# Sentinel rows written once ahead, and last expert tiles that overlap their neighbour

## The reference

```python
h = tok(x)                       # convolution over 5 frames, relu, batch norm over all rows
h = h + attn(layernorm(h))       # 8 heads, 121 keys per sequence, a column bias from 8192 edges
h = h + ffn(layernorm(h))        # below

logits = xf @ Wr + br            # xf: 3872 x 128, 8 experts
idx = top_1(logits)              # the gate is softmax over one value, so 1
for e in range(8):               # W1[e] 128 x 512, W2[e] 512 x 128
    oe = relu(xf @ W1[e] + b1[e]) @ W2[e] + b2[e]
    out = out + where(idx == e, oe, 0)
```

## Time and profile before

| | us |
|---|---|
| three runs | 348.50, 352.64, 356.53 |
| profiled execution | 345.34 |
| its span | 343.6 |
| PE busy | 275.7 (80%) |
| ACT busy | 227.0 (66%) |
| DVE busy | 225.4 (66%) |
| POOL busy | 213.2 (62%) |
| mean granted TensorE clock | 0.916 |

### The profile page before, as it was taken

The page is one execution under the profiler, slowest core; times in us unless marked ns, Lnnn a source line. Parts: engine busy times, 40 slices in busy tenths (PEclk is TensorE's granted clock), DMA queues, the critical chain, the costliest instruction groups (busy, mean ns, idle before and its releaser), DMA issues. The chain is left out here.

```text
span 343.6 us, 7885 instructions
## 1 busy us (share of the span) xinstructions
PE 275.7 (80%) x2139; PEld 215.0 (63%) x2139; DVE 225.4 (66%) x714; ACT 227.0 (66%) x843; POOL 213.2 (62%) x299
## 2 busy tenths in 40 slices
PE   3890969899999998897898879856008999999980
PEld 2660746556767665665656656545007999999970
DVE  2895676888988999877787686455403565656540
ACT  3851378889888998697897788640005777777740
POOL 7044554787766867888888886667721454545551
PEclk9995698999999999999999999895557999999996
DMA  3200990000000000001000100112634333333300
GB/s 94 79 2 1 303 281 18 0 2 1 3 0 2 1 3 15 16 15 32 15 24 23 31 15 17 30 31 73 171 98 122 93 101 109 94 104 108 91 13 0
DMA packets 15579, 19.15 MB, mean 56 GB/s; under 512 B 3960, under 2 KB 11676, under 8 KB 15537
## 3 DMA queue, kind: packets, MB, share of 16 engines
q1 hardware_dynamic: 11520, 11.73, 12.1%
q0 software_dynamic: 3296, 5.98, 6.0%
q10 hardware_dynamic: 720, 0.94, 0.9%
HBM read 10.69 MB, written 8.44 MB: 56 GB/s over the span
## 5 line engine op out<-in xcount | busy, mean ns | idle before, releaser
L467 ACT ACTIVATE P<-psS,nmax 121x121 f32<-121x121 f32 x256 | 88.9, 380 | 17.9 <-DVE nmax L709 17.2
L929 PE MATMUL psS<-patT,qT 128*121 128x484 f32 x128 | 64.3, 607 | 2.5 <-ACT P L467 1.7
L396 POOL DMA_INDIRECT out<-y_out,xg x38 | 36.9, 971 | 46.9 <-issue 31.5
L362 POOL TENSOR_TENSOR P<-P,rden 121x968 f32<-121x968 f32 x31 | 56.5, 1823 | 8.2 <-DVE rden L781 7.6
L467 ACT ACTIVATION_READ_ACCUMULATOR P<-psS,nmax 121x1 f32 x256 | 57.4, 224 | 0.0
L835 DVE TENSOR_SCALAR hT<-psT,b1T 128x128 f32<-128x128 f32 x76 | 23.3, 347 | 46.7 <-PE psT L1062 46.6
L709 DVE TENSOR_REDUCE nmax<-psS 121x4 f32<-121x484 f32 x64 | 41.5, 651 | 15.0 <-PE psS L929 15.0
L941 PE MATMUL psT<-ident,P 121*121 121x121 f32 x256 | 34.4, 277 | 15.2 <-POOL P L362 13.2
L941 PEld LDWEIGHTS psT<-ident,P 121*121 121x121 f32 x256 | 29.7, 185 | 21.9 <-POOL P L362 19.2
L374 POOL DMA_INDIRECT region_d<-rows,pos x32 | 34.9, 1091 | 8.8 <-issue 8.8
L476 ACT ACTIVATE PT<-psT 121x968 f32<-121x968 f32 x32 | 32.0, 1000 | 12.6 <-PE psT L941 12.6
(11 more groups left out here) (210 smaller groups left out, 620.4 us busy)
## 6 DMA issues: line engine op xcount, KB each, us to landing
xg<-region_d SPq DMA_DIRECT2D x38, 128.5 KB
W_sb<-in_L_ffn_W SPq DMA_DIRECT2D x1, 2048.0 KB, 9.2
region_d<-pads SPq DMA_DIRECT2D x11, 128.5 KB, 4.3
out<-y_out,xg POOLq DMA_INDIRECT x38
region_d<-pads ACTq DMA_DIRECT2D x4, 128.5 KB
b_bc<-in_L_ffn_b SPq DMA_DIRECT2D x1, 512.0 KB, 5.9
region_d<-rows,pos POOLq DMA_INDIRECT x32
xs<-in_x ACTq DMA_DIRECT2D x1, 402.5 KB, 3.9
```

Source lines behind the costliest of these rows:

```text
L362: pool.tensor_tensor(P[0:L, i % 2, :, :], P[0:L, i % 2, :, :], rden[0:L, i % 2, :].unsqueeze(2).to_broadcast([L, H, L]), ALU.mult).then_in ...
L396: pool.indirect_dma_start(out, bass.IndirectOffsetOnAxis(xg[:, u, 2 * D:ROW].bitcast(I32), 0), y_out[:, u, :], None, bounds_check=N - 1, o ...
L467: ins = act.activation(P[0:L, t % 2, h, :], psS[0:L, h // HG, h % HG * L:(h % HG + 1) * L], ACT.Exp, bias=nmax[0:L, h:h + 1], accum_out=de ...
L929: pe.matmul(psS[0:L, g, 0:HG * L], qT[:, t // 2 % 2, g, t % 2 * L:t % 2 * L + L], kbd[:, t % 4, g, :], start=True, stop=True).then_inc(s_S, 1)
```

## The change

The sentinel rows no longer depend on the counts. SP writes them once, behind the weights: 128 rows at the head of each expert's region in one DMA, and seven tiles behind the regions in a second. Row scatters overwrite the heads afterwards, so POOL waits for both DMAs (`d_pads` 32) and for the row numbers. `write_pads` is gone from SP and ACT.

An expert's last tile now starts 128 rows before the end of its rows, or at the region's head if it has fewer than 128, and so overlaps the tile ahead. VectorE's table computes that limit (`lim`, `dlim`) and takes the smaller of the plain start and the limit. `again` is how many rows a tile repeats; a matmul spreads it over partitions, and `mask` holds 8192 where a row is a repeat. For each tile VectorE joins row numbers and mask (`sidx`), and the store skips those rows as it skips sentinels. The number of tiles and both tile loops stay as they are. On PE two small matmuls of the row ends go, and one for the mask comes.

```diff
--- before.py
+++ after.py
@@ -170,11 +170,17 @@
         cnt = sb("cnt", [1, 3, E])
         cmpt = sb("cmpt", [1, E, B - 1])
         tscan = sb("tscan", [1, E])
-        pad_row = sb("pad_row", [1, E], I32)
-        past = sb("past", [1, 2, NT, E])
-        tab = sb("tab", [1, 2, NT])
+        base_e = sb("base_e", [1, E])
+        lim = sb("lim", [1, E + 1])
+        dlim = sb("dlim", [1, 2, E])
+        past = sb("past", [1, 3, NT, E])
+        tab = sb("tab", [1, 4, NT])
         eid = sb("eid", [1, NT], I32)
         row0 = sb("row0", [1, NT], I32)
+        again = sb("again", [1, NT], BF16)
+        part0 = sb("part0", [128, 1])
+        mask = sb("mask", [128, NT], I32)
+        sidx = sb("sidx", [128, NT], I32)
 
         xg = sb("xg", [128, RING, ROW])
         xgT = sb("xgT", [128, 2, 128])
@@ -207,9 +213,9 @@
             sem, "s_v1 s_r1 s_nm1 s_xn s_h0b s_kbd s_v2 s_r2".split())
         s_carry_p, s_carry_v = sem("s_carry_p"), sem("s_carry_v")
         s_top = sem("s_top")
-        r_oh, r_sum, r_seen, r_rank, r_pick, r_pos, r_cnt, r_start, r_chain, r_eid, r_row = map(
-            sem, "r_oh r_sum r_seen r_rank r_pick r_pos r_cnt r_start r_chain r_eid r_row".split())
-        d_rows, d_pads, d_extra = sem("d_rows"), sem("d_pads"), sem("d_extra")
+        r_oh, r_sum, r_seen, r_rank, r_pick, r_pos, r_cnt, r_chain, r_eid, r_row, r_again, r_mask, f_si = map(
+            sem, "r_oh r_sum r_seen r_rank r_pick r_pos r_cnt r_chain r_eid r_row r_again r_mask f_si".split())
+        d_rows, d_pads = sem("d_rows"), sem("d_pads")
         s_pads, s_rowid = sem("s_pads"), sem("s_rowid")
         f_ld = [sem(f"f_ld{u}") for u in range(RING)]
         f_sca = [sem(f"f_sca{u}") for u in range(RING)]
@@ -228,14 +234,6 @@
 
             return 0 <= t - back < n
 
-
-        def write_pads(eng, experts):
-
-            eng.wait_ge(s_pads, 2)
-            eng.wait_ge(r_start, 1)
-            for e in experts:
-                first = eng.value_load(pad_row[0:1, e:e + 1], min_val=e * CAP, max_val=e * CAP + N)
-                eng.dma_start(region_d[bass.ds(first, 128), :], pads[:, :]).then_inc(d_pads, 16)
 
         block = ctx.enter_context(nc.Block())
 
@@ -263,14 +261,13 @@
                          W2.rearrange("e (c h) o -> h (e c) o", h=128)).then_inc(l_ffn, 16)
             sp.dma_start(b1_in[:, :], b1.rearrange("e (c h) -> (e c) h", h=128)).then_inc(l_ffn, 16)
             sp.wait_ge(s_pads, 2)
-            for n in range(XT):
-                sp.dma_start(region_d[E * CAP + n * 128:E * CAP + (n + 1) * 128, :], pads[:, :]).then_inc(d_extra, 16)
-
-            write_pads(sp, range(0, E // 2))
+            sp.dma_start(region_d[0:E * CAP, :].rearrange("(e r) c -> r e c", r=CAP)[0:128, :, :],
+                         pads[:, :].unsqueeze(1).to_broadcast([128, E, ROW])).then_inc(d_pads, 16)
+            sp.dma_start(region_d[E * CAP:E * CAP + XT * 128, :].rearrange("(n r) c -> r n c", r=128),
+                         pads[:, :].unsqueeze(1).to_broadcast([128, XT, ROW])).then_inc(d_pads, 16)
 
             sp.wait_ge(d_rows, 16 * B)
-            sp.wait_ge(d_pads, 16 * E)
-            sp.wait_ge(d_extra, 16 * XT)
+            sp.wait_ge(d_pads, 32)
             sp.wait_ge(r_row, 1)
             for s in range(NT):
                 u = s % RING
@@ -321,7 +318,10 @@
                                pattern=[[128 // EG, EG]], channel_multiplier=-1).then_inc(s_power, 1)
             pool.iota(col_iota[:, :], pattern=[[1, EF * EG]], base=1, channel_multiplier=0, **fl).then_inc(s_colio, 1)
             pool.iota(base_row[:, :, :], pattern=[[0, 4], [CAP, E]], base=0, channel_multiplier=0, **fl).then_inc(s_colio, 1)
+            pool.iota(part0[:, :], pattern=[[0, 1]], base=0, channel_multiplier=1, **fl).then_inc(s_colio, 1)
             pool.memset(seen[:, 0, :], 0.0).then_inc(s_colio, 1)
+            pool.iota(base_e[:, :], pattern=[[CAP, E]], base=0, channel_multiplier=0, **fl).then_inc(s_colio, 1)
+            pool.memset(lim[:, E:E + 1], float(E * CAP + XT * 128)).then_inc(s_colio, 1)
             pool.memset(pads[:, 0:2 * D], 0.0).then_inc(s_pads, 1)
             pool.iota(pads[:, 2 * D:ROW].bitcast(I32), pattern=[[0, 1]], base=NOROW, channel_multiplier=0).then_inc(s_pads, 1)
             pool.iota(rows[0:L, :, 2 * D:ROW].bitcast(I32).rearrange("p b a -> p (b a)"), pattern=[[L, B]], base=0,
@@ -374,6 +374,8 @@
                 pool.indirect_dma_start(region_d, bass.IndirectOffsetOnAxis(pos[0:L, b:b + 1], 0), rows[0:L, b, :], None,
                                         bounds_check=E * CAP - 1, oob_is_err=False).then_inc(d_rows, 16)
 
+            pool.wait_ge(s_rowid, 1)
+            pool.wait_ge(d_pads, 32)
             pool.wait_ge(l_rows, 16 * N_ROWS)
             norm1(0)
             norm1(1)
@@ -392,8 +394,9 @@
 
             for s in range(NT):
                 u = s % RING
+                pool.wait_ge(f_si, s + 1)
                 pool.wait_ge(f_y, s + 1)
-                pool.indirect_dma_start(out, bass.IndirectOffsetOnAxis(xg[:, u, 2 * D:ROW].bitcast(I32), 0), y_out[:, u, :], None,
+                pool.indirect_dma_start(out, bass.IndirectOffsetOnAxis(sidx[:, s:s + 1], 0), y_out[:, u, :], None,
                                         bounds_check=N - 1, oob_is_err=False).then_inc(f_sca[u], 16)
             for u in range(RING):
                 pool.wait_ge(f_sca[u], 16 * len(range(u, NT, RING)))
@@ -496,8 +499,6 @@
 
             act.wait_ge(f_b1, 1)
             act.activation(b1T[:, :], psT[:, 0, 0:E * FC], ACT.Identity).then_inc(f_b1T, 1)
-
-            write_pads(act, range(E // 2, E))
 
             act.wait_ge(r_eid, 1)
             act.wait_ge(f_b1T, 1)
@@ -795,12 +796,20 @@
                 link(ins, r_chain, rl)
 
             dve.wait_ge(r_cnt, 1)
-            dve.tensor_copy(pad_row[0:1, :], psU[0:1, E:2 * E]).then_inc(r_start, 1)
             ne, tiles, skip = (cnt[0:1, n, :] for n in range(3))
-            rlink(dve.tensor_copy(ne, psU[0:1, 0:E]))
-            rlink(dve.tensor_tensor(cmpt[0:1, :, :], ne.unsqueeze(2).to_broadcast([1, E, B - 1]),
-                                    tile_starts[0:1, :].unsqueeze(1).to_broadcast([1, E, B - 1]), ALU.is_gt))
-            rlink(dve.tensor_reduce(tiles, cmpt[0:1, :, :], AX.X, ALU.add))
+            dve.tensor_copy(ne, psU[0:1, 0:E]).then_inc(r_chain, 1)
+            rl[0] += 1
+            dve.tensor_scalar(dlim[0:1, 0, :], psU[0:1, 0:E], -128.0, 0.0, ALU.add, ALU.max).then_inc(r_chain, 1)
+            rl[0] += 1
+            dve.wait_ge(r_chain, 1)
+            dve.tensor_tensor(cmpt[0:1, :, :], ne.unsqueeze(2).to_broadcast([1, E, B - 1]),
+                              tile_starts[0:1, :].unsqueeze(1).to_broadcast([1, E, B - 1]), ALU.is_gt).then_inc(r_chain, 1)
+            rl[0] += 1
+            dve.wait_ge(r_chain, 2)
+            rlink(dve.tensor_tensor(lim[0:1, 0:E], dlim[0:1, 0, :], base_e[0:1, :], ALU.add))
+            dve.tensor_reduce(tiles, cmpt[0:1, :, :], AX.X, ALU.add).then_inc(r_chain, 1)
+            rl[0] += 1
+            rlink(dve.tensor_tensor(dlim[0:1, 1, :], lim[0:1, 1:E + 1], lim[0:1, 0:E], ALU.subtract))
             dve.tensor_scalar(skip, tiles, -128.0, float(CAP), ALU.mult, ALU.add).then_inc(r_chain, 1)
             rl[0] += 1
             rlink(dve.tensor_tensor_scan(tscan[0:1, :], ones_e[0:1, :], tiles, 0.0, ALU.mult, ALU.add))
@@ -808,10 +817,23 @@
                                     tile_iota[0:1, :].unsqueeze(2).to_broadcast([1, NT, E]), ALU.is_le))
             dve.tensor_reduce(tab[0:1, 0, :], past[0:1, 0, :, :], AX.X, ALU.add).then_inc(r_chain, 1)
             rl[0] += 1
-            rlink(dve.tensor_tensor(past[0:1, 1, :, :], past[0:1, 0, :, :], skip.unsqueeze(1).to_broadcast([1, NT, E]), ALU.mult))
+            dve.tensor_tensor(past[0:1, 1, :, :], past[0:1, 0, :, :], skip.unsqueeze(1).to_broadcast([1, NT, E]),
+                              ALU.mult).then_inc(r_chain, 1)
+            rl[0] += 1
+            dve.wait_ge(r_chain, rl[0] - 1)
             dve.tensor_scalar(eid[0:1, :], tab[0:1, 0, :], float(E - 1), None, ALU.min).then_inc(r_eid, 1)
-            rlink(dve.tensor_reduce(tab[0:1, 1, :], past[0:1, 1, :, :], AX.X, ALU.add))
-            dve.tensor_tensor(row0[0:1, :], tab[0:1, 1, :], tile_rows[0:1, :], ALU.add).then_inc(r_row, 1)
+            dve.tensor_tensor(past[0:1, 2, :, :], past[0:1, 0, :, :], dlim[0:1, 1, :].unsqueeze(1).to_broadcast([1, NT, E]),
+                              ALU.mult).then_inc(r_chain, 1)
+            rl[0] += 1
+            dve.wait_ge(r_chain, rl[0])
+            rlink(dve.tensor_reduce(tab[0:1, 1:3, :], past[0:1, 1:3, :, :], AX.X, ALU.add))
+            rlink(dve.tensor_tensor(tab[0:1, 3, :], tab[0:1, 1, :], tile_rows[0:1, :], ALU.add))
+            dve.scalar_tensor_tensor(out=row0[0:1, :], in0=tab[0:1, 2, :], scalar=lim[0:1, 0:1], in1=tab[0:1, 3, :],
+                                     op0=ALU.add, op1=ALU.min).then_inc(r_row, 1)
+            dve.wait_ge(r_row, 1)
```

(15 more changed lines are left out.)

## The result

The change makes the kernel slower: 372.75 us median (371.65 to 377.83, 4 runs) against 350.57 us (348.16 to 356.53, 4 runs), a ratio of 1.0647 with the 95% interval [1.0517, 1.0776]. That is 22.2 us by the medians; 23.9 were forecast. The forecast time was 376.5, its range 368 to 384. The ratios here are taken over undisturbed runs alone and the medians over all, so the two can differ by up to 1% and even in sign.

The account below looks back on a forecast made before the run. TensorE was taken to bound the tiles, and POOL's start of `norm1(0)` the front. Terms 25.6 - 1.9 + 0.15 gave plus 23.9 us on the median of 352.64, so 376.5 us, range 368 to 384.

Parts of the forecast that it names:

- The stall: POOL's new wait ahead of `norm1(0)`: the fill lands at 58.1, so attention starts later, plus 25.6 us (23.5 to 27).
- No cover and no slack given back: PE, ACT and VectorE all wait behind POOL; nothing hides the delay and later stages return none of it.
- The clock adds nothing: Granted clock restarts at the same 0.50 after the longer idle time: zero, with 1.5 us either way.
- `write_pads`, minus 1.9: End of attention: without SP's sentinel tiles, row scatters release the first tile load sooner, minus 1.9 us (0 to 2.4).
- Table and mask, 0: VectorE's table 1.6 us longer, mask under 1.1 us, both hidden before the first tile: 0.
- sidx, 0.15: 38 VectorE ops in the tile stage, hidden by PE's cadence except the last: plus 0.15 us (0 to 5.7).
- The sum: All terms over the whole kernel: 25.6 - 1.9 + 0.15 = plus 23.9 us.
- The wait costs nothing: Rival, POOL ahead of `norm1(0)`: fill landed by 32.5 us, time 350.9, not slower; chance 0.03.
- Much less: Rival: unseen slack in the front, or attention regaining 10 us or more, gives 360 to 367; chance 0.04.
- far slower fill: Rival: the 15 tiles move at half of 228 GB/s, land at 66.5, plus 8.4 us, 385; chance 0.06.
- VectorE late: Rival, tile stage: the full 5.7 us of `sidx` falls on the cadence, 382; chance 0.02.

Follow-up runs that it names:

- e2: Kernel before plus one line: POOL waits for its seven early sentinel tiles ahead of `norm1(0)`; 370.1 us, ratio 1.0708.
- e1: Changed kernel with POOL's wait for the fill moved from ahead of `norm1(0)` to ahead of the first row scatter; 349.12 us, ratio 1.0045.
- e3: Changed kernel with both fills issued ahead of SP's wait for the gather, POOL's wait left ahead of `norm1(0)`; 348.76 us, ratio 1.0053.
- e4: Changed kernel with both fills directly behind SP's wait for the gather, ahead of W1, W2 and b1; 362.22 us, ratio 1.0443.
- e6: Kernel before, unchanged, run again for a second profile; 343.94 us in one execution.
- e8: Kernel before with row scatters two loop steps sooner (step t scatters image t - 14), nothing of the change; 350.65 us, ratio 1.0050.
- e9: Kernel before with both early fills in the front and POOL's wait ahead of `norm1(0)`; old table, no mask, `write_pads` kept; 349.30 us, ratio 1.0015.
- e10: Repeat of the changed kernel with both fills ahead of SP's wait for the gather; 350.14 us, ratio 1.0088.
- e5: Changed kernel with fills ahead of SP's gather wait, plus `sidx` issued five times per tile, four into a spare buffer; 349.82 us, ratio 0.9956.

## Why the prediction was right

The time came to 372.75 us where 376.5 was forecast. Of these 3.75 us, 2.1 lie in the base, the median of 352.64 that the fourth run brought to 350.57, and 1.7 in the sum (23.9 against 22.2).

**The stall**, forecast 25.6 us (23.5 to 27), measured 24.67 in the profile. Issue at 46.8 and 47.2 and landing at 57 came as said; e2 shows the wait alone enough, e1 and e3 that 0.3 to 0.4 us of it are left when the wait or the fill is moved. Inside the term two errors offset each other, so that it came so close was in part luck. In e2, where attention stands still as well, the seven tiles landed 8.25 us after their first issue (47.38 to 55.63); in the changed kernel that would be 55.0, where I took 53.5. The fifteen landed 10.35 us after the first issue (46.78 to 57.13), so the eight more cost 2.1 us, where I took 4.6. 1053 KB in 2.1 us would be 500 GB/s, more than any window above, so part of it is the merging: the seven single tiles moved at 319, 223, 176, 109 and 59 GB/s in the microseconds from 49 to 54 (e2), the merged fill at 331 for three. The weights' 4211 KB were through at about 48.8 and the fill's 1974 KB at about 56, which is 274 GB/s; I had 228 from the stretch with seven small tiles. The Trainium skill's figure for a 1 MB transfer ("DMA: Bandwidth & Descriptors", Bandwidth), 341 GB/s, measured there on loads into SBUF, is nearer to the measured 331 of 49 to 52 us than my row was; over the whole fill the measurement is below it.

**No cover and no slack given back**: right. PE waited 30.80 us, ACT and VectorE with it, and e4 gives the loss in proportion (13.9 us of delay, 14.1 of time).

**The clock adds nothing**: right for the restart (0.50 before and after the stall in both profiles), too simple for the rest. The spread of 1.5 us either way that I allowed is small against the 7.8 us between single runs of the kernel before (344.31 to 352.12).

**`write_pads`, minus 1.9**: the mechanism was read off one execution and was wrong in part. SP's slow steps of about 0.7 us did not come back in e2, e6, e8 and e9. What stays is a landing of the last scatter that is 0.4 to 2.6 us sooner. From the start of the last scatter to the first tile load it is 3.99 to 6.14 us in the five profiles with `write_pads` and 3.83 in the changed kernel, so the gain is 0.2 to 2.3 us, inside my bounds of 0 and 2.4. The top of it needs the shorter lag of e8; the closest pair, e9 and e10, gives 0.16.

**Table and mask, 0**: they are hidden as worked out. The table takes 1.1 us longer (from VectorE's first read of the counts to `row0` 4.59 us, 3.53 before), where I had 1.6. In the changed kernel `row0` is done at 274.88, 8.4 us before the scatters release SP, and the mask at 275.73. **sidx, 0.15**: each takes 0.150 us, and five of them per tile change nothing measurable.

**The sum** came out at 23.9 against 22.2 measured. But with the wait made harmless the sum says 1.75 us faster, and the three comparisons say slower: 0.6 to 2.5 us by the medians, 0.45 to 0.88% by the ratios, 0.2 to 0.8 us at equal clock. That step failed: the small terms do not add up to a gain. The term that was mis-sized is the 1.9 us for `write_pads`, 0.16 in the closest pair. Another part lies outside the span (373.45 - 371.5 = 1.95 us around it, 345.34 - 343.6 = 1.74 before), 0.2 us. The rest is not settled. A direct trial without the mask was not made, because repeated rows would then be stored twice with nothing to order the writes.

**The rivals.** "The wait costs nothing" came true in another kernel, e3. "Much less" is refuted by e2 and e4, whose losses follow the delay in full; "far slower fill" and "VectorE late" by the landing at 57 and by e5.

## What to carry to other kernels

A wait moved to the front of an engine's program is priced by when the last byte that it waits for lands, so ask where the transfer stands in its queue before asking how long it is. Place such a wait where its data is first used, or issue the transfer before the heavy traffic: either way it cost 1 us or less here by the medians, while the wait ahead of `norm1(0)`, for a transfer behind the weights, cost 22. Before pricing the removal of a chain by one profile, take a second: here the chain's slow steps existed in one of five executions. And compare small differences at equal clock.

## What the runs showed of the hardware

- One DMA of 1028 KB and one of 900 KB moved 331 GB/s together over their first 3 us and 274 over the whole 1974 KB. Seven of 128.5 KB in a row began at 319 to 325 GB/s for a microsecond and came to 205 over 4.5 us.
- The same second fill of 900 KB landed 9.7 us after issue behind the weights' tail, 11.9 us with W1 issued 0.6 us later, and 11.5 us in the front with nothing large behind it. That W1 shared the engines is shown by the bytes; what it cost is not.
- A single program on one core has a spread of 7.8 us (344.3 to 352.1, 80 runs) that goes with the mean granted clock, 0.918 to 0.896, by 2.4 us per 0.01; comparisons of under 1% need the clock of each run beside its time.
- Register, load and issue steps on SP took about 0.7 us each for ten microseconds in one execution; in four others the same issues took 0.33 to 0.40.
